# Four matmuls into an unused bank at the end of step 12 of the first attention

## What is computed

```python
x = L0_attn_x                                  # 8 x 512 x 128
xn = _layernorm(x, axis=-1)
s = _L0_attn_ref(xn, ...)                      # 16 heads of 8 features, softmax over all 512 keys
g = _silu(_L0_ffn_ref(xn, ...))                # 128 -> 512 -> 512 -> 512 -> 128, gelu between
x = x + s * g
# layers 1 to 3: the same shape with other attentions and feed-forwards
```

## Time and profile before

| | |
|---|---|
| median of 3 runs | 4274.97 us |
| the profiled execution, as timed | 4280.27 us |
| its span, first to last instruction | 4276.5 us |
| mean granted TensorE clock | 0.929 of full speed |
| TensorE matmuls busy | 3483.5 us (81%) |
| VectorE busy | 2665.2 us (62%) |
| ScalarE busy | 1828.8 us (43%) |
| GpSimd busy | 830.4 us (19%) |

### The profile page before, as it was taken

One profiled execution on the slowest core, in us unless ns is written; L12 is line 12 of the kernel. 1 busy time (PEld: TensorE's weight loads), 2 busy tenths in 40 slices (PEclk: granted clock), 3 DMA queues, 4 the chain that ended last, 5 costly groups with the idle time before them and its releaser, 6 DMA issues. The chain is left out here.

```text
span 4276.5 us, 55101 instructions
## 1 busy us (share of the span) xinstructions
PE 3483.5 (81%) x19186; PEld 1807.3 (42%) x19303; DVE 2665.2 (62%) x5636; ACT 1828.8 (43%) x3753; POOL 830.4 (19%) x721
## 2 busy tenths in 40 slices
PE   4887798878987888877988889888888779887857
PEld 1344434444344443444444453444434444444424
DVE  4576656666476655766557664766557665566645
ACT  1444444444433534444444444335344444444414
POOL 1022300331012400223002310124002230023113
PEclk9999999999998999999999999999999999989978
DMA  4000101001011010000010010110100000100130
GB/s 152 29 13 26 35 30 33 31 4 62 3 33 33 1 64 29 13 26 35 30 33 28 6 60 5 33 33 1 64 29 12 26 35 30 33 29 5 60 84 21
DMA packets 87839, 139.93 MB, mean 33 GB/s; under 512 B 12472, under 2 KB 62466, under 8 KB 85002
## 3 DMA queue, kind: packets, MB, share of 16 engines
q1 hardware_dynamic: 81042, 127.30, 9.3%
q10 hardware_dynamic: 6522, 9.06, 0.7%
HBM read 106.14 MB, written 29.39 MB: 32 GB/s over the span
## 5 line engine op out<-in xcount | busy, mean ns | idle before, releaser
L625 DVE TENSOR_REDUCE nmax<-banks 128x1 f32<-128x512 f32 (+3 forms) x1216 | 760.2, 658 | 412.7 <-PE banks L449 249.7
L545 ACT ACTIVATE probs<-banks 128x512 f32<-128x512 f32 (+3 forms) x1024 | 478.3, 525 | 314.6 <-PE banks L467 311.2
L449 PE MATMUL banks<-ks,qs 72*128 72x512 bf16 (+3 forms) x1536 | 466.3, 350 | 116.5 <-DVE nmax L625 88.0
L467 PE MATMUL banks<-qs,ks 74*128 74x512 bf16 (+3 forms) x1536 | 470.1, 343 | 55.5 <-ACT probs L545 20.4
L94 PE MATMUL banks<-filler,identb 128*128 128x512 bf16 x1296 | 364.2, 395 | 28.9 <-PEq L74 21.2
L449 PEld LDWEIGHTS banks<-ks,qs 72*128 72x128 bf16 x1536 | 147.2, 103 | 445.9 <-DVE nmax L625 267.4
L545 ACT ACTIVATE early<-banks 128x256 f32<-128x256 f32 (+3 forms) x512 | 196.5, 439 | 222.0 <-PE banks L467 221.8
L510 PE MATMUL banks<-probs,v 128*32 128x512 f32 (+3 forms) x2048 | 244.4, 550 | 40.0 <-POOL probs L591 30.7
L1299 ACT ACTIVATE probs<-banks,nm 128x192 f32<-128x192 f32 x512 | 173.2, 422 | 237.5 <-DVE nm L1251 237.5
L264 POOL TENSOR_TENSOR rstd<-var,neghalf 128x4 f32<-128x4 f32 (+1 forms) x16 | 21.2, 1324 | 1281.5 <-DVE var L215 1151.8
L467 PEld LDWEIGHTS banks<-qs,ks 74*128 74x128 bf16 x1536 | 142.6, 101 | 259.6 <-ACT probs L545 81.4
(11 more groups left out here) (463 smaller groups left out, 6725.5 us busy)
## 6 DMA issues: line engine op xcount, KB each, us to landing
qs<-parts_scratch SPq DMA_DIRECT2D x300, 96.0 KB
ks<-parts_scratch SPq DMA_DIRECT2D x288, 96.0 KB
parts_scratch<-parts SPq DMA_DIRECT2D x50, 384.0 KB, 2.5
shared<-in_w_h SPq DMA_DIRECT2D x17, 1024.0 KB, 7.3
shared<-in_w SPq DMA_DIRECT2D x25, 256.0 KB, 4.1
qs<-max_parts SPq DMA_DIRECT2D x192, 4.0 KB
xn<-in_x SPq DMA_DIRECT2D x9, 256.0 KB, 2.6
factor_scratch<-g SPq DMA_DIRECT2D x9, 256.0 KB, 2.2
```

The lines of the kernel that those rows point to most:

```text
L449: mm = nc.tensor.matmul(K.ps[:, b, i * keys:(i + 1) * keys], K.qs[0:72, 4 * g + j, t * P:(t + 1) * P], K.ks[0:72, 4 * g + j, 0:keys], star ...
L467: nc.tensor.matmul(K.ps[:, b, q0:T], K.ks[0:KR, h, k * P:(k + 1) * P], K.qs[0:KR, h, q0:T], start=True, stop=True).then_inc(scored2, 1)
L545: nc.scalar.activation(probs[:, 4 * (q % QUADS) + m % 4, q0:T], K.ps[:, bank("second", m), q0:T], ACT.Exp, scale=scale).then_inc(exped, 1)
L625: nc.vector.tensor_reduce(nmax[:, t, h:h + len(heads)], K.ps[:, n % 2, 0:len(heads) * keys].rearrange("p (j k) -> p j k", k=keys), AX.X, A ...
```

## The change

A table `FILLED` is added to the work that runs beside an attention: step -> (bank, number of matmuls). It is empty except in `TernaryFfn`, which names step 12, bank 5, four matmuls. On TensorE, after the scores of the step and after its `weigh` part (there is none in step 12), `attention` looks the step up and issues the matmuls. No wait and no signal is added, and nothing is moved.

```diff
@@ class Beside
     FILLERS_FROM = 0
+
+    FILLED = {}
     started = False
@@ attention, block.tensor
                         mm.then_inc(weighed, 1)
+                    if s in beside.FILLED:
+                        keep_busy(nc, K, *beside.FILLED[s])
                     beside.run(beside.on_tensor, s)
@@ class TernaryFfn
     LAST_STEP = 12
+    FILLED = {12: (5, 4)}
     OUT_STEP = 36
```

## The result

The changed kernel takes 4227.5 us (median of four runs, 4224.9 to 4231.9) against 4276.3 us before: a ratio of 0.9888, with a 95% interval of 0.9876 to 0.9901.

The account below looks back on a forecast made before the run. TensorE alone was taken to set the pace in the slow stretch behind the exponential's table load. 4280.27 - 31.9 + 0 = 4248.4 us profiled, 5.30 us above the median, so 4243.1 us; range 4232 to 4262 us.

Parts of the forecast that it names:

- What bounds the stretch and what the fall costs: Behind the exponential's table load TensorE alone sets the pace; falls in seven batches cost 31.9 us over batch 0.
- The price of the fillers: Four matmuls ending step 12, 0.86 us a batch, priced at 0 because VectorE's 0.59 us and TensorE's wait cover them.
- the reserve: Cover left over at step 12 once VectorE's 0.59 us of idle time takes up the fillers' delay: 0.02 us.
- Whether they hold the clock: Fillers ahead of the first `weigh` part keep the clock at 1.00, bounded between no effect and batch 0.
- The upper end: Bound taken for the fillers' effect: clock 1.00 behind the exponential's table load, as in batch 0 over the same instructions.
- The rests: Seven stretches from Silu's load to the exponential's next load, summing to 3088.95 us; 12 us more or 7 us less possible.
- Holding in part: Behind step 12 the fall stays in three or four of seven batches, half the gain left: 4259 us; chance 0.16.
- short waits have no part in it: The 0.70 us wait before the fall does not lower the clock; time stays 4275 us, or 4282; chance 0.08.
- The slower rival: Clock already down when step 12's fillers are issued, each taking twice as long: 4284 us, up to 4289; chance 0.03.

Follow-up runs that it names:

- e5: The changed kernel with one VectorE delay of 0.72 us and three more matmuls in each batch, at the end of the first attention: 4236.3 us, ratio 0.9911.
- e12: The changed kernel with six more matmuls ahead of TensorE's 1.98 us wait in step 2 of layer 2's attention: 4253.6 us, ratio 0.9949.
- e13: The kernel before with four VectorE delays, 2.88 us a batch, and added matmuls at the end of the first attention: 4286.3 us, ratio 1.0025.

## Why the prediction was wrong, point by point

- **What bounds the stretch and what the fall costs.** Right. All seven attentions came to 53.35 us, 31.8 us less in sum, forecast 31.9.
- **The price of the fillers.** Right in its sum: the first score came 0.57 us late and nothing was added from load to load (53.35 us against 53.34). One step was not as told. VectorE's idle time did not go to 0; it came two maxima earlier and was 0.45 us long, still under the 0.59 us. So the reserve was 0.14 us and not 0.02. With eight fillers each batch pays 0.70 us, and in step 8, where nothing covers them, the full 0.88.
- **Whether they hold the clock.** Right, though it was a choice between two bounds and no row showed it. The upper end, batch 0, was the value. How little is needed was not foreseen: one filler is enough in seven of eight batches, and removing the wait does the same.
- **The rests.** This step failed. The prediction held them at their sum of 3088.95 us and gave them 12 us up and 7 us down; they came to 3069.4 us, 19.5 less, and 2.8 us more went behind the last batch, where the prediction had no term. The mechanism was named ("later falls are dealt anew"), but the term was mis-sized, and its lower end was not the shortest row's: it put all rests at the 440.29 us of batch 0, while batch 5 stood in the rows with 437.13. Seven such rests would be 29 us less, a lower end of 4214 us, and it would have held the measured 4227.5. The shortest rest looked like an exception; in the changed kernel six of seven are 438.1 to 438.3 us. That all of them fell on the short side was not to be read from the rows: with 0.72 or 1.44 us of delay the same kernel loses 9 or 21.5 us of the gain.
- **The rivals.** Holding in part did not occur with four fillers, though it did with one. That short waits have no part in it is out: where the table load and its wait of 0.70 us were removed, no batch fell. The Trainium skill's rule on long gaps ("TensorE: Matmul & The Clock Gate", section "Why this matters for your kernels") does not cover this case; no gap near the falls was longer than 0.70 us. The same page's section "A second HAM failure mode: psum-queue depth-cycling" describes short idle times between groups of matmuls that bring the clock down, and with that the runs agree: seven of eight batches fell behind the 0.70 us, none without it. The wait alone doesn't decide: batch 0 and all batches with two fillers have it and hold. The slower rival never came into play: the clock was 1.00 when the fillers were issued. Its mechanism is real, as step 14 shows, where four fillers took 1.90 us instead of 1.03.

**What stays open.** Which falls of the rests go at which moment was not traced one by one; the runs show that they move with the timing, not a rule by which a rest's length could be told ahead. Nor is it shown why batch 0 falls with one filler and not with none. That the rows of a filler don't matter was shown in this place alone.

## What to carry to other kernels

Where TensorE sets the pace and its clock falls behind a short wait, a few fillers into an unused bank, put ahead of the wait and inside the slack of the engine that reads the next result, are worth a try; here they gave 4.5 us in each of seven batches. Behind the wait they came too late, and beyond the slack they cost most of their own length. Look first where the clock falls: in layer 2 it fell ahead of the wait that was filled, and nothing was gained. Where a clock falls in many places, a change of a batch's length, even a delay, can re-deal the later falls: take the range for the unchanged rest from the shortest and the longest row, times the number of batches, and judge an edit by its own stretch, not by the total.

## What the runs showed of the hardware

One matmul of 512 columns, 0.22 us, decided over a stretch of about 10 us at 1.2 GHz and 4.5 us of time in seven batches. Four matmuls with 72 rows held the clock as well as four with 128. A delay of 0.72 us in each of 8 batches, with three matmuls beside it, left the kernel before as fast as it was (4275.3 against 4274.4 us). Batches did not come in all lengths: in twelve of the sixteen profiled kernels each of batches 1 to 6 took 491.5, 494.9, 498.3 or 501.7 us, to within 0.2 us (the others are the kernel before, e5, e12 and e13), and going from 1.44 to 2.88 us of delay in the changed kernel left it at 494.9.
